# One SBUF input per VectorE step, and a new order of work in each slot, in an audio tower kernel

## What is computed

```python
tokens = einsum('bnpd,edp->bne', patches, Wr) + b                    # 64 x 93 x 128
xn = layernorm(tokens) * gamma + beta
q, k, v = (conv3(w1 @ xn) for w1, conv3 in ((wq1, wqd), (wk1, wkd), (wv1, wvd)))   # 8 heads x 64
attn = softmax(q @ k.T * scale + alibi, causal)                      # 93 x 93 per head
h = tokens + (attn @ v) @ wout.T
x = layernorm(h); logits = x @ gate_weight.T                         # 16 experts
top_vals, top_idx = top_k(logits, 2); routing_w = softmax(top_vals)
y_mean[e] = w2[e] @ (mean over the tokens of e of silu(w1[e] @ x))
out = h + sum_k routing_w[k] * y_mean[top_idx[k]]
```

## Time and profile before

| | |
|---|---|
| median of 3 runs | 791.71 us (791.15 to 791.81) |
| the profiled execution | 791.94 us, of it the traced span 790.3 us |
| busy: TensorE / VectorE / ScalarE / GpSimd | 706.6 / 605.4 / 607.5 / 382.8 us |
| steps with all six stages on, t = 5 to 15 | about 127 to 536 us of the span |
| the pipeline drains, t = 16 to 19 | about 536 to 650 us |
| experts' tiles and output | from about 650 us |
| granted TensorE clock over the span | 0.971 of full speed |

### The profile page before, as it was taken

One profiled execution on the slowest core, in us unless ns is written; L12 is line 12 of the kernel. 1 busy time (PEld: TensorE's weight loads), 2 busy tenths in 40 slices (PEclk: granted clock), 3 DMA queues, 4 the chain that ended last, 5 costly groups with the idle time before them and its releaser, 6 DMA issues.

```text
span 790.3 us, 21100 instructions
## 1 busy us (share of the span) xinstructions
PE 706.6 (89%) x6514; PEld 626.4 (79%) x6514; DVE 605.4 (77%) x1579; ACT 607.5 (77%) x2022; POOL 382.8 (48%) x390
## 2 busy tenths in 40 slices
PE   4789999989998999999898989888888778999986
PEld 4678898878787888888797878776677577999983
DVE  2167778887888888888888798887887558888865
ACT  3557898978887888888787978787886757899960
POOL 3642434756556465565565656554362565122200
PEclk9889999999999999999999999999998969999996
DMA  5522124322211121211212122102124112122205
GB/s 181 146 79 60 48 87 145 103 78 61 59 51 50 48 54 45 53 49 49 64 40 64 49 52 55 47 12 68 26 78 164 32 48 68 52 69 63 63 19 156
DMA packets 44273, 53.99 MB, mean 68 GB/s; under 512 B 13651, under 2 KB 31251, under 8 KB 43696
## 3 DMA queue, kind: packets, MB, share of 16 engines
q1 hardware_dynamic: 30048, 38.84, 17.2%
q0 software_dynamic: 12544, 12.87, 6.1%
q10 hardware_dynamic: 1616, 1.48, 0.6%
HBM read 42.69 MB, written 10.26 MB: 67 GB/s over the span
## 4 chain that ended last, share of the span: by engine, by line
PE 36%; DVE 34%; ACT 18%; issue 8%; DMA 2%; POOL 1%; SPq 1%; DVEq 0%; ACTq 0%
ACT prob L805 12%; DVE qkv L979 6%; DVE qkv L982 5%; DVE prob L1095 4%; PE psSO L707 4%; PE psTP L707 4%; PE psTP L451 4%; DVE rmin L1065 4%; PE psTP L453 3%; PE psTP L452 3%; DVE sel L1161 3%; PE psSO L652 3%; PE psTP L523 3%; ACT qkv L785 3%; PE psSO L542 3%
## 5 line engine op out<-in xcount | busy, mean ns | idle before, releaser
L1326 POOL DMA_INDIRECT expert_rows<-hn,slot x128 | 174.7, 1365 | 74.8 <-DVE slot L1174 44.8
L805 ACT ACTIVATE prob<-psSO,rmin 93x93 f32<-93x93 f32 x512 | 151.8, 354 | 20.8 <-DVE rmin L1065 20.8
L1259 POOL TENSOR_TENSOR x_lo<-x_raw,x_hi 128x752 fp32r<-128x752 f32 x64 | 115.0, 1797 | 52.5 <-ACT x_hi L777 52.0
L785 ACT ACTIVATE qkv<-psTP,taps 128x372 f32<-128x372 f32 x192 | 112.5, 586 | 21.8 <-PE psTP L453 21.1
L979 DVE SCALAR_TENSOR_TENSOR qkv<-psTP,taps,qkv 128x368 f32<-128x368 f32 x192 | 112.6, 586 | 20.3 <-ACT qkv L785 20.3
L982 DVE SCALAR_TENSOR_TENSOR qkv<-psTP,taps,qkv 128x364 f32<-128x364 f32 x192 | 114.5, 596 | 6.8
L451 PE MATMUL psTP<-x_hi,wtok_hi 128*128 128x376 f32 x256 | 98.9, 386 | 11.1 <-DVE wtok_lo L967 9.1
L805 ACT ACTIVATION_READ_ACCUMULATOR prob<-psSO,rmin 93x1 f32 x512 | 98.2, 192 | 0.0
L451 PE MATMUL psTP<-xnT_hi,wqkv_hi 128*128 128x372 f32 x192 | 80.3, 418 | 17.8 <-DVE qkv L982 17.7
L453 PE MATMUL psTP<-x_hi,wtok_lo 128*128 128x376 f32 x256 | 87.6, 342 | 0.0
L452 PE MATMUL psTP<-x_lo,wtok_hi 128*128 128x376 f32 x256 | 87.5, 342 | 0.0
(11 more groups left out here) (194 smaller groups left out, 1730.2 us busy)
## 6 DMA issues: line engine op xcount, KB each, us to landing
x_raw<-in_x SPq DMA_DIRECT2D x64, 376.0 KB, 3.2
w1s<-in_w POOLq DMA_DIRECT2D x8, 512.0 KB, 4.9
w<-in_w SPq DMA_DIRECT2D x4, 1024.0 KB, 6.0
out<-resid SPq DMA_DIRECT2D x16, 160.0 KB, 2.7
xsE<-expert_rows SPq DMA_DIRECT2D x36, 64.0 KB, 2.1
xs<-expert_rows SPq DMA_DIRECT2D x36, 64.0 KB, 1.8
xs<-expert_rows POOLq DMA_DIRECT2D x36, 64.0 KB, 2.1
expert_rows<-hn,slot POOLq DMA_INDIRECT x128, 3.5
```

The costliest lines, as they stand in the source:

```text
L785: nc.scalar.activation(qkv[u][:, k, :, :], psP[(k + 1) % 2][:, 0:GT].rearrange("p (b n) -> p b n", n=NT), ACT.Copy, scale=taps[:, k, 2:3]) ...
L805: i = nc.scalar.activation(prob[:, a, hh, :], psS[:NT, a, hh * NT:(hh + 1) * NT], ACT.Exp, bias=rmin[:, a, hh:hh + 1], scale=-1.0, accum_o ...
L1259: nc.gpsimd.tensor_tensor(x_lo[u][:, 0:PIECE], x_raw[u][:, :], x_hi[u][:, 0:PIECE].bitcast(F32), ALU.subtract)\
L1326: nc.gpsimd.indirect_dma_start(rows, bass.IndirectOffsetOnAxis(slot[1 - u][:, c:c + 1], 0), hn[1 - u][:, c % GB, :], None)\
```

## The change

VectorE's steps read at most one input from SBUF. `idxf`, `wden`, `wts`, `slotf`, `rden` and the ranks (`pos` is gone, the ranks stay in `psRank`) now lie in PSUM, in columns of `psO` and `psS` that were unused at that time; `gap`, `mask` and the last sum of `rw` are reductions of one operand where they were sums or differences of two. Since `rden` and the row sums lie beside the scores, `scores` now waits for `prob_ready` (the scaling) where it waited for `rden_done`, and the transposes of the gate wait for `rw_done` as well. `early_piece`'s links and `max_index` are as they were.

The order of work in a slot is another one on all four engines. The two halves of `turn_prob` are apart, with the scores between them.

In the orders below, brackets stand for work that is there in some slots only.

```diff
                 wait(pe, exp_done, n * 2)
-                wait(pe, rden_done, n)
+                wait(pe, prob_ready, n)
...
                     if f.gate and s == 2:
                         wait(pe, hn_ready, t - 3)
                         wait(pe, base_done, t - 4)
+                        wait(pe, rw_done, t - 4)
...
                     if f.attn:
                         dve.wait_ge(exp_done, n * 2 + 2)
-                        nc.vector.reciprocal(rden[:, :, :], psS[:NT, :, 4 * NT:4 * NT + 4]).then_inc(rden_done, 1)
-                    if f.gate and s == 3:
-                        rank(t - 4, u)
+                        nc.vector.reciprocal(rden, den).then_inc(rden_done, 1)
                     if f.attn:
                         dve.wait_ge(rden_done, n + 1)
                         nc.vector.tensor_tensor(prob[:, :, :, :], prob[:, :, :, :],
-                                                rden[:, :, :].unsqueeze(3).broadcast_to([NT, 2, 4, NT]),
+                                                rden.unsqueeze(3).broadcast_to([NT, 2, 4, NT]),
                                                 ALU.mult).then_inc(prob_ready, 1)
...
-                nc.vector.tensor_tensor(gap[:, :], top[:, :, 1], top[:, :, 0], ALU.subtract).then_inc(gap_done, 1)
+                nc.vector.tensor_reduce(gap[:, :], top[:, :, 0:2], AXX, ALU.subtract).then_inc(gap_done, 1)
...
-                nc.vector.tensor_tensor(mask[:, :].rearrange("p (b e) -> p b e", e=E), hot[:, 0:GB, :],
-                                        hot[:, GB:, :], ALU.add).then_inc(mask_done, 1)
+                with nc.allow_low_precision(reason="sums of zeros and ones"):
+                    nc.vector.tensor_reduce(mask[:, :], hot[:, :, :].rearrange("p (k b) e -> p (b e) k", k=2), AXX, ALU.add)\
+                        .then_inc(mask_done, 1)
...
-                nc.vector.tensor_tensor(pos[:, :].rearrange("p (b e) -> p b e", e=E),
+                nc.vector.tensor_tensor(psRank.rearrange("p (b e) -> p b e", e=E),
...
-                nc.vector.tensor_scalar(wden[:, :], egap[:, :], 1.0, None, ALU.add).then_inc(wden_done, 1)
+                nc.vector.tensor_scalar(wden, egap[:, :], 1.0, None, ALU.add).then_inc(wden_done, 1)
...
                 nc.vector.tensor_tensor(sel[:, :, :].rearrange("p (k b) e -> p k (b e)", k=2),
                                         hot[:, :, :].rearrange("p (k b) e -> p k (b e)", k=2),
-                                        pos[:, :].unsqueeze(1).broadcast_to([NT, 2, GB * E]), ALU.mult)\
+                                        psRank.unsqueeze(1).broadcast_to([NT, 2, GB * E]), ALU.mult)\
...
-                nc.vector.tensor_tensor(rw[:, :, 0:E], wsel[:, 0:GB, :], wsel[:, GB:, :], ALU.add).then_inc(rw_done, 1)
+                nc.vector.tensor_reduce(rw[:, :, 0:E], wsel[:, :, :].rearrange("p (k b) e -> p b e k", k=2), AXX, ALU.add)\
+                    .then_inc(rw_done, 1)
```

More of the change, by code:

```diff
@@ L1099, in step @@
                         conv(t, u, 3 * s + 1)
-                    if isinstance(t, int) and t == NG + 2 and s == 3:
-                        first_weights()
+                    if f.gate and s == 2:
+                        route(t - 4)
                     if prev:
@@ L1105, in step @@
                         nc.vector.tensor_tensor(res, psWout, res, ALU.add).then_inc(res_add, 1)
+                    if f.gate and s == 3:
+                        rank(t - 4, u)
                     if f.proj:
                         conv(t, u, 3 * s + 2)
-                    if f.gate and s == 2:
-                        route(t - 4)
+                    if isinstance(t, int) and t == NG + 2 and s == 3:
+                        first_weights()
                     if isinstance(t, int) and t == NG + 3 and s == 0:
```

226 lines of the change are left out of this document (116 added, 110 removed).

## The result

The changed kernel takes **804.96 us** (median of 4 runs, 803.66 to 805.97), beside 791.76 us for the kernel before on the same chip: a ratio of 1.0142, 95% interval 1.012 to 1.0165. The prediction was 783 us, with a range of 769 to 796 us. The profiled execution took 805.97 us, of it 804.2 us span, 13.9 us more than the 790.3 us before.

What follows compares the result with a forecast made beforehand. The prediction took a ring of waits between the engines, lengthened by VectorE stalls, to bound the kernel. Its terms, -15.6 us in t = 6 to 14 the largest, summed to -8.5 us: 791.7 - 8.5 = 783 us, range 769 to 796 us.

Steps and rivals of the forecast that it cites:

- the stalls: VectorE's sel, gap and slot 2 scaling, lengthened beside GpSimd's x_lo in full steps: 3.90 us a step.
- the ring: Engines waiting on each other in each slot, scaling to scaling; 32.83 us for four slots in the drain.
- the 7.2 us slot of t = 18: Forecast for each slot of t = 18, where nothing covers the scores' wait for the scaling; 6.12 us before.
- two runs: Two runs of fp32r matmuls a slot on TensorE: 0.7 us a step of its work saved, counted as 0.
- I take all 3.90 us a step as gone.: Full steps: one SBUF input per VectorE step, and wden in PSUM, remove the whole stall; 35.1 us in t = 6 to 14.
- 32.83 + 3.90 = 36.73: Full step: four slots of the drain plus the stall, set against 37.13 us measured; 0.40 us left over.
- The forecast step, 35.4 us: Full step after the change: 32.83 + 0.40 + 2.04 = 35.3 us, with 0.1 for slot 3.
- So every slot gets 0.51 us longer, 2.04 us a step.: Every slot: ScalarE's vrow, moved ahead of the last exponentials, lies between row minimum and reciprocal.
- covered by 0.7 us: Full steps: scores, now waiting for the scaling, are ready 1.7 us behind it, VectorE's row minimum comes at 2.4 us.
- Rival 2: Slot 3 of full steps: route delays the third convolution and xn transposes, making the kernel slower; chance 0.18 for slower.
- the rest of the program loses about 7 us: Rival 2's sum outside the full steps; with it, slower is decided once a full step exceeds 36.3 us.
- Step 18 ... four slots like it, +4.2 us.: t = 18, without convolutions to cover the scores' wait: slots go from 6.12 to 7.2 us.

Runs made afterwards that it cites:

- e11: e10 with two runs of fp32r products a slot in place of four, by moving TensorE's products; 764.34 us.
- e2: The kernel before in its own order with all new operands, rden in PSUM too, so the scores wait for the scaling; 769.42 us.
- e8: The changed kernel with vrow behind the last exponentials and the second projection product ahead of the first tap product; 775.21 us.
- e7: The changed kernel with, in t = 18, rden in SBUF and scores ahead of the transposes, waiting for the reciprocal only; 797.43 us.
- e5: The changed kernel with the residual sum ahead of route in slot 2; 804.76 us.
- e12: The changed kernel with the edits of e8 and e7, and route behind the row minimum of slot 3; 764.03 us.
- e13: The changed kernel with products whose result is thrown away on TensorE in t = 18, no wait changed; 798.45 us.
- e1: The kernel before in its own order with the new operands, except rden kept in SBUF, so scores wait for the reciprocal; 775.76 us.
- e10: e2 with rden in SBUF and scores waiting for the reciprocal only from t = 17, and route behind slot 3's row minimum; 756.45 us.

## Why the prediction was wrong, point by point

**The mechanisms named were there; the sum had two of their sizes wrong and left the clock out.** Right: the stalls, that the operands remove them, the price of 0 for a PSUM operand of the scaling (0.92 to 0.93 us both ways), `vrow`'s 0.50 us where only the ring runs (slot 1 of t = 16, 7.76 to 8.26 us), and the 7.2 us slot of t = 18 at full clock. That two runs are worth nothing is not contradicted (e11), but no run had them alone. The Trainium skill (Perfetto Trace Analysis, "Optimizing Scalar/DVE Operations") gives VectorE about 60 ns of overhead for SBUF and about 125 ns for PSUM; the scaling's rows don't show the difference. The cause is a little wider than `x_lo`: `sel` in t = 10 starts at 315.91, 0.73 us before `x_lo`, beside an indirect DMA's instruction (315.33 to 316.61).

**"I take all 3.90 us a step as gone."** They were gone from the rows, and e2 shows 37.13 - 34.34 = 2.79 us gone from the step. `sel` stands between the row minimum and the reciprocal, where VectorE waits for ScalarE anyway; 1.06 of its 2.43 us lay in that wait. The cross-check that seemed to confirm it, 32.83 + 3.90 = 36.73, compared a full step with the drain. There slot 0 of t = 17 takes 7.76 us, and in e2's full steps, without any stall, 8.73. Two errors of about 1.1 us cancelled: the stalls were taken too high, the step without them too low (32.83 + 0.40, where e2 has 34.34). The forecast step, 35.4 us, was short by 0.87: 1.11 us from this, less 0.21 from the next point, to rounding.

**"So every slot gets 0.51 us longer, 2.04 us a step."** The order's whole cost in a step is 36.27 - 34.34 = 1.93 us, close to the 2.14 put down, but it is made up otherwise: 0.41 for `vrow`, 1.28 for the second product that comes late, 0.24 for the rest, which is all in slot 3 (9.65 us in e8, 9.38 in e2). The 0.41 is the least sure of these: e7, with the changed kernel's code up to t = 17, has 35.95 us a step, 0.32 less, and nothing explains it. The prediction took the exponentials to follow `vrow` with nothing else to wait for, so the nearness of the two sums is luck. It asked whether the scores' wait was covered up to the row minimum ("covered by 0.7 us"), and not whether the work queued behind the scores was. That is where the wait came out.

**Rival 2, slot 3.** Its link is close to the right one: in the changed kernel TensorE waits in slot 3 for the residual sum behind `route`, and with the sum moved it waits as long for the convolution behind `route` (e5). Moving `route` off the ring then takes slot 3 from 9.65 us (e8) to 9.11 (e12). It put the point from which it decides at 36.3 us a step, which the kernel just reached. But most of the loss lies elsewhere: "the rest of the program loses about 7 us" came out at 21.5 us.

**"Step 18 ... four slots like it, +4.2 us."** The wait and `vrow` together cost 4.0 us (e13). The step that failed is that the sum held TensorE's clock as it was: the term that was missing is the clock, 6.65 us. The trace of before could have warned: its granted clock is 0.58 in the window from 600 us, and the prediction's own link makes TensorE idle about a microsecond more in each slot of a stretch with no filling work. t = 17 lost 2 us more than predicted as well, in slot 3 (11.18 us), in which the granted clock is 0.69; with the sum ahead of `route` (e5) that slot takes 9.60, at 1.00. How much of it is the clock stays open: in the old order the slot takes 9.17 us at 0.66 (the kernel before) and at 1.00 (e1).

**The ends.** The first scaling came 2.8 us later, not 0.3. With the changed kernel's fill it starts anywhere from 68.09 to 70.70 us, in the old order from 66.23 to 67.80 us (e10 and e1), and e8 and e12, with the product first, have 68.01 and 67.58. So the new fill costs something, and how much of the 2.8 us is the spread of executions is open. Behind the last scaling, the statistics of the last group do come 2.4 us earlier (8.85 us behind it in place of 11.24), but the first gathered tile is fetched 51.02 us behind the last scaling, where it was 49.94. What holds the fetch wasn't tested, so the cause of these 3.3 us of the miss stays open.
